# A fused attention and FP4 feed-forward kernel: semaphores per weight load, and the diagonal chunk of attention moved from first to last

## What is computed

```python
xn = _layernorm(x, axis=-1)
s = _L0_attn_ref(xn, Wq, bq, Wk, bk, Wv, bv, ln_g, ln_b, Wo, bo)
g = _silu(_L0_ffn_ref(xn, w_gate, w_up, w_down))
x = x + s * g
```

```python
def fp4_quant_dequant(x):                 # blocks of 16 along the last dim
    scale = jnp.maximum(jnp.max(jnp.abs(xb), axis=-1, keepdims=True) / 6.0, 1e-12)
    xn = xb / scale
    idx = jnp.searchsorted(_MID, jnp.abs(xn))       # 7 thresholds
    return (_GRID[idx] * jnp.sign(xn) * scale).reshape(shape)
gate = fp4_linear(x, w_gate);  y = fp4_linear(x, w_up)    # w_gate, w_up: [2816, 1024]
h = jax.nn.silu(gate) * y
return fp4_linear(h, w_down)                               # w_down: [1024, 2816]
```

## Time and profile before

| | us |
|---|---|
| median of 2 timed runs | 7727.67 |
| the two runs | 7749.9 and 7705.45 |
| the profiled execution, its own time | 7301.52 |
| span of its slowest core | 7299.9 |
| spans of its 8 cores | 7263.4 to 7299.9 |
| busy in that span: TensorE, VectorE, ScalarE, GpSimd | 3961.0, 2938.6, 798.3, 289.5 |
| mean granted TensorE clock of the cores (of 2.4 GHz) | 0.768 to 0.774 |

### The profile page before, as it was taken

How to read it: one execution, slowest core, us unless ns; L and a number is a source line. 1 busy time by engine, 2 the same in 40 slices (tenths; PEclk the granted TensorE clock), 3 DMA queues, 4 the chain that set the end, 5 groups by cost and what they waited for, 6 DMA issues and landing times.

```text
span 7299.9 us, 35941 instructions; the slowest of 8 cores (7263.4 to 7299.9 us)
## 1 busy us (share of the span) xinstructions
PE 3961.0 (54%) x10160; PEld 1770.9 (24%) x10160; DVE 2938.6 (40%) x7271; ACT 798.3 (11%) x1294; POOL 289.5 (4%) x420
## 2 busy tenths in 40 slices
PE   2600000000366774687577467857765688767746
PEld 1300000000122332232233223223332232223322
DVE  1177777777524562001456300033651000145630
ACT  1100000000030000023000002320000023300000
POOL 0000000000020000001000000100000000000000
PEclk9755555555688887798888778878887799988877
DMA  3110111011101111110111011002111200011102
GB/s 97 33 46 29 52 46 40 34 47 48 51 6 52 69 35 32 58 32 3 56 55 49 24 58 39 0 10 71 46 35 40 73 9 0 6 52 62 42 24 60
DMA packets 140128, 296.00 MB, mean 41 GB/s; under 512 B 10016, under 2 KB 77728, under 8 KB 139936
## 3 DMA queue, kind: packets, MB, share of 16 engines
q0 software_dynamic: 52480, 207.63, 8.6%
q1 hardware_dynamic: 87456, 86.08, 3.9%
HBM read 250.70 MB, written 42.99 MB: 40 GB/s over the span
## 4 chain that ended last, share of the span: by engine, by line
PE 43%; DVE 28%; DMA 10%; DVEq 6%; ACT 5%; issue 4%; ACTq 1%; POOL 1%; PEldq 1%; SPq 0%; PEld 0%; POOLq 0%
PE p L996 9%; PE p L950 6%; DVEq L83 6%; PE p L957 5%; PE p L709 5%; DMA ffnw<-wdq_s 4%; PE p L717 4%; PE p L854 3%; PE p L617 3%; PE p L657 3%; DMA xbuf<-x 3%; DVE qfm L280 3%; DVE qfm L285 2%; PE p L335 2%; PE p L383 2%
## 5 line engine op out<-in xcount | busy, mean ns | idle before, releaser
L950 PE MATMUL p<-ffnw,xnfm 128*128 128x512 f32 (+1 forms) x1536 | 722.2, 630 | 503.8 <-DMA ffnw<-wuq_s 317.0
L335 PE MATMUL p<-ident,hqfm 128*128 128x128 f32 (+1 forms) x592 | 133.7, 402 | 1457.6 <-DVE hqfm L306 1450.6
L996 PE MATMUL p<-hqfm,ffnw 128*128 128x512 f32 x1408 | 682.3, 648 | 340.8 <-DMA ffnw<-wdq_s 340.8
L957 PE MATMUL p<-ffnw,xnfm 128*128 128x512 f32 (+1 forms) x1536 | 620.2, 557 | 0.0
L724 DVE COPY ftmp<-p 65x512 f32<-65x512 f32 x32 | 22.0, 687 | 1397.4 <-PE p L717 1397.4
L950 PEld LDWEIGHTS p<-ffnw,xnfm 128*128 128x128 f32 x1536 | 331.1, 219 | 876.3 <-issue 865.7
L996 PEld LDWEIGHTS p<-hqfm,ffnw 128*128 128x128 f32 x1408 | 292.0, 210 | 729.4 <-issue 729.4
L335 PEld LDWEIGHTS p<-ident,hqfm 128*128 128x128 f32 (+1 forms) x592 | 103.5, 214 | 1488.2 <-issue 1483.4
L709 PE MATMUL p<-probs,vT 128*65 128x512 f32 x640 | 360.6, 716 | 151.9 <-POOL hqfm L686 79.2
L1009 DVE TENSOR_TENSOR sfm<-ftmp,sfm 128x512 f32<-128x512 f32 x32 | 22.1, 692 | 1005.2 <-ACTq L83 1005.2
L957 PEld LDWEIGHTS p<-ffnw,xnfm 128*128 128x128 f32 x1536 | 291.8, 190 | 312.7 <-issue 306.1
(11 more groups left out here) (153 smaller groups left out, 4908.7 us busy)
## 6 DMA issues: line engine op xcount, KB each, us to landing
ffnw<-wdq_s POOLq DMA_DIRECT2D x32, 1408.0 KB, 8.7
xbuf<-x SPq DMA_DIRECT2D x80, 512.0 KB, 4.0
ffnw<-wgq_s POOLq DMA_DIRECT2D x20, 2048.0 KB, 9.6
ffnw<-wuq_s POOLq DMA_DIRECT2D x20, 2048.0 KB, 14.1
ffnw<-Wq SPq DMA_DIRECT2D x32, 512.0 KB, 5.4
ffnw<-Wo SPq DMA_DIRECT2D x32, 512.0 KB, 4.4
hqfm<-wg POOLq DMA_DIRECT2D x22, 512.0 KB, 5.1
hqfm<-wu POOLq DMA_DIRECT2D x22, 512.0 KB, 4.9
```

The source lines that it names most:

```text
L335: E.do("tensor", lambda e, s=s, pb=pb, j=j, bp=bp, rows=rows: e.transpose(pb[:, j * rows:(j + 1) * rows], s, ident[bp:bp + rows, bp:bp + r ...
L950: E.do("tensor", lambda e, pg=pg, kc=kc, qt=qt, hw=hw: e.matmul(pg[:, 0:hw], xnfm[:, kc * 512 + qt * 128: kc * 512 + qt * 128 + 128], ffnw ...
L957: E.do("tensor", lambda e, pu=pu, kc=kc, qt=qt, hw=hw: e.matmul(pu[:, 0:hw], xnfm[:, kc * 512 + qt * 128: kc * 512 + qt * 128 + 128], ffnw ...
L996: E.do("tensor", lambda e, pd=pd, hc=hc: e.matmul(pd[:, 0:512], wdbuf[:, hc * 128:(hc + 1) * 128], hqfm[:, hc * 512:(hc + 1) * 512], start ...
```

## The change

Three edits.

1. In PW, both DMAs of unit k go on one of four semaphores (`qG`, `qG1` and two new ones, `qP0` and `qP1`), chosen by k mod 4, and the waits of ScalarE and VectorE ahead of unit k name that semaphore with the count kept at its own load.
2. For `wd`, both DMAs of tile oc go on `qG` (even) or `qG1` (odd), and the waits name that semaphore with the count of the tile's own load.
3. In the C stages the chunks run in ascending order, `for ch in range(qc + 1)`, so that the diagonal chunk is the last. `start` and `stop` of the AV accumulation and the waits for the free banks follow this order.

```diff
@@ -24,7 +24,7 @@
 HBS = [(0, 512), (512, 512), (1024, 512), (1536, 512), (2048, 512), (2560, 256)]
 R6 = float(np.float32(1.0) / np.float32(6.0))
 
-SEMS = ["qC", "qX0", "qX1", "qW0", "qW1", "qO0", "qO1", "qG", "qG1", "qGW", "qGW1",
+SEMS = ["qC", "qX0", "qX1", "qW0", "qW1", "qO0", "qO1", "qG", "qG1", "qP0", "qP1", "qGW", "qGW1",
         "t2v", "t2s", "t2g", "v2t", "v2s", "v2q", "v2g", "vv",
         "s2t", "s2v", "s2q", "s2g", "g2t"]
 
@@ -448,6 +448,8 @@
         qg_cnt = [0] * NU
         qg1_cnt = [0] * NU
 
+        SEM4 = ("qG", "qG1", "qP0", "qP1")
+
         def pw_load(k):
             w_src = units[k][0]
             h0, hw, hcl0 = units[k][3], units[k][4], units[k][5]
@@ -457,9 +459,8 @@
                 w_in = buf[:, ci * 1024:ci * 1024 + 1024]
                 E.do("gpsimd", lambda e, w_in=w_in, hc=hc, w_src=w_src: e.dma_start(
                     out=w_in, in_=w_src[hc * 128:(hc + 1) * 128, :]),
-                    sem=("qG" if ci == 0 else "qG1"), n=16)
-            qg_cnt[k] = E.c["qG"]
-            qg1_cnt[k] = E.c["qG1"]
+                    sem=SEM4[k % 4], n=16)
+            qg_cnt[k] = E.c[SEM4[k % 4]]
 
         for k in range(3):
             pw_load(k)
@@ -469,10 +470,8 @@
         for k in range(NU):
             w_src, w_dst, hb, h0, hw, hcl0 = units[k]
             buf = RING[k % 5]
-            E.wait("scalar", "qG")
-            E.wait("scalar", "qG1")
-            E.wait("vector", "qG")
-            E.wait("vector", "qG1")
+            E.wait("scalar", SEM4[k % 4], qg_cnt[k])
+            E.wait("vector", SEM4[k % 4], qg_cnt[k])
             quant_group(pw_items([buf[:, 0:1024], buf[:, 1024:2048]], 1024))
             E.wait("tensor", "v2s")
             wst = wstage_ab[wsa]
@@ -510,24 +509,23 @@
 
         def wd_load(oc):
             stag = wd_stag[oc % 2]
+            sm = "qG" if oc % 2 == 0 else "qG1"
             E.do("gpsimd", lambda e, oc=oc, stag=stag: e.dma_start(
                 out=stag[:, 0:1408], in_=wd[oc * 128:(oc + 1) * 128, 0:1408]),
-                sem="qG", n=16)
+                sem=sm, n=16)
             E.do("gpsimd", lambda e, oc=oc, stag=stag: e.dma_start(
                 out=stag[:, 1408:2816], in_=wd[oc * 128:(oc + 1) * 128, 1408:2816]),
-                sem="qG1", n=16)
-            wd_qg[oc] = E.c["qG"]
-            wd_qg1[oc] = E.c["qG1"]
+                sem=sm, n=16)
+            wd_qg[oc] = E.c[sm]
 
         E.wait("gpsimd", "t2g")
         wd_load(0)
         wd_load(1)
         for oc in range(NKC):
             stag = wd_stag[oc % 2]
-            E.wait("scalar", "qG")
-            E.wait("scalar", "qG1")
-            E.wait("vector", "qG")
-            E.wait("vector", "qG1")
+            sm = "qG" if oc % 2 == 0 else "qG1"
+            E.wait("scalar", sm, wd_qg[oc])
+            E.wait("vector", sm, wd_qg[oc])
             for grp in range(2):
                 subs = [stag[:, (grp * 2 + i) * 704:(grp * 2 + i + 1) * 704] for i in range(2)]
                 quant_group(pw_items(subs, 704))
@@ -642,12 +640,8 @@
                     hA = g * NKV + hkp
                     hB = hA + 1
                     chq = hA // 2
-                    ch_order = [qc] + list(range(qc))
-                    nch = len(ch_order)
-                    for ci, ch in enumerate(ch_order):
+                    for ch in range(qc + 1):
                         diag = ch == qc
-                        first = ci == 0
-                        last = ci == nch - 1
                         for j in range(4):
                             kc = ch * 4 + j
                             bA = SCA[j % 2]
@@ -700,26 +694,26 @@
                             E.wait("tensor", "g2t")
                         else:
                             E.wait("tensor", "s2t")
-                        if first:
+                        if ch == 0:
                             E.wait("tensor", av4_free[0][0], av4_free[0][1])
                             E.wait("tensor", av5_free[0][0], av5_free[0][1])
                         for j in range(4):
                             kc = ch * 4 + j
                             slot = (hkp * 16 + kc) * 65
-                            E.do("tensor", lambda e, j=j, slot=slot, first=first, last=last: e.matmul(
+                            E.do("tensor", lambda e, j=j, slot=slot, ch=ch: e.matmul(
                                 ps[4][0:65, 0:512],
                                 vT[:, slot:slot + 65],
                                 probs[:, j * 512:(j + 1) * 512],
-                                start=(first and j == 0), stop=(last and j == 3)))
+                                start=(ch == 0 and j == 0), stop=(diag and j == 3)))
                         for j in range(4):
                             kc = ch * 4 + j
                             slot = ((hkp + 1) * 16 + kc) * 65
-                            E.do("tensor", lambda e, j=j, slot=slot, first=first, last=last: e.matmul(
+                            E.do("tensor", lambda e, j=j, slot=slot, ch=ch, diag=diag: e.matmul(
                                 ps[5][0:65, 0:512],
                                 vT[:, slot:slot + 65],
                                 probsB[:, j * 512:(j + 1) * 512],
-                                start=(first and j == 0), stop=(last and j == 3)),
-                                sem=("t2v" if (last and j == 3) else None))
+                                start=(ch == 0 and j == 0), stop=(diag and j == 3)),
+                                sem=("t2v" if (diag and j == 3) else None))
                     E.wait("vector", "t2v")
                     E.do("vector", lambda e: e.tensor_copy(av_sbA[0:65, 0:512], ps[4][0:65, 0:512]),
                          sem="v2t")
```

## The result

| | before | changed |
|---|---|---|
| median of all timed runs, us | 7363.85 (10 runs) | 7375.13 (11 runs) |
| lowest and highest run | 7304.89, 7805.44 | 7129.47, 7685.45 |
| the profiled execution, its own time | 7301.52 | 7144.55 |
| ratio of comparable runs | | 0.9766, interval 0.9707 to 0.9826 |

Some executions of either kernel are stretched by up to 8% by a lower granted clock on one half of the chip's cores, so that the medians of all runs mix both kinds and hide the gain, while the ratio and the two profiled executions leave the stretched ones out. By the ratio the kernel is 2.3% faster, and since the interval reaches 0.9826, a gain of a little under 2% can't be excluded.

What follows compares the result with a forecast made beforehand. PW was taken as a serial loop in which each unit waits for a load just issued. Savings of 150.5 us (waits) and 13.6 us (chunk order), 164.1 in sum, off the 7727.7 us median gave 7563.6 us; range 7500 to 7640.

Steps and rivals of the forecast that it cites:

- The waits of the loads: In PW, each unit or `wd` tile waiting only for its own load was to save 150.5 us.
- Unit 0: First PW unit: Abs was to start near 344.3 instead of 349.71, no longer waiting for load 3; 5.4 us.
- Tile 0 of `wd`: First `wd` tile in PW: waiting for its own load instead of two was to save some 3.4 us.
- The chunk order: C1 to C3, diagonal chunk last: worth 0 by waits, a gain of 13.6 us by the granted clock.
- bounds +48 and -62: C1 to C3: C2's worst pattern in all 24 groups loses 48 us; all clock falls gone gains 62.
- full-clock groups: Groups of C1 to C3 without a clock fall were worked out as 29.81, 43.22 and 56.63 us.
- I let the fall of the even chunk go and keep the other: C2: the clock fall behind the 1.51 us stall goes, that behind the mask's 2.46 us stays; 8 x 1.70 us.
- C2's excess: C2: groups of 47.80 us against 43.22 at full clock, 4.58 us a group, 36.6 us over 8 groups.
- Clock worse in C: Rival, C stages: groups with one clock fall get two, leaving 102.5 us saved, 7625 us; chance 0.29.
- All falls gone: Rival, C1 to C3: every clock fall vanishes, saving 212.8 us in all, 7515 us; chance 0.06.
- GpSimd and VectorE collide: Rival, PW: DMA issues beside VectorE's units cost 50.2 us, leaving 114 saved, 7614 us; chance 0.05.
- Slower: Rival, C1 to C3: TensorE stays at 1.2 GHz through whole bursts, 7857 us with 40 of them; chance 0.02.

Runs made afterwards that it cites:

- loads_only: The changed kernel with its new semaphore waits on weight loads but the chunk loop of the kernel before; ratio 0.9814 to before, profiled execution 7226.0 us.
- all_three: The changed kernel plus useless matmuls filling the C stages' stalls and down-projection loads in two halves of `ffnw`; profiled execution 6770.7 us.
- two_newer: The changed kernel, with ScalarE and VectorE also waiting ahead of unit k for the load of unit k+2; execution 7606.6 us, PW 1445.5 us.

## Why the prediction was right or wrong

**The time itself was wrong, by its last step.** The range of 7500 to 7640 us missed the measured 7375.13. The step that failed is the one that took the saving off 7727.7: "The two timed runs have a median of 7727.7, 426 us above it, which no view explains". Of the ten runs of before, four lie above 7700, these two among them, and six between 7304.89 and 7369.17, beside the profiled execution's 7301.5. The other figure of the same paragraph, 7137 us on the scale of the profiled execution, has 7144.6 as its answer. Two timed runs that stand 5.5 and 6.1% above a profile are a warning that they are of another kind; a range on one of the two scales holds the time only by luck, and the saving of 164 us should have been put on the profile's. The median of all ten runs would not have saved the forecast: 7363.85 - 164.1 is 7199.8. Of the eleven runs after, six took 7375.13 us or more, so their median is set by how many of them are long, and not by the change.

**The saving was right.** Forecast 164.1, measured 156.9 between the two profiled executions; 0.9775 by the profile's scale, 0.9766 measured.

**The waits of the loads.** Forecast 150.5 us. Of it 145.1 fall behind the first Abs: measured -146.2, and -149 in loads_only. The period of a unit was to be 42.41 and is 42.25, that of a tile 60.70 and is 60.75. Unit 0 was to start some 0.37 us behind VectorE's last copy and not 5.8: its Abs starts at 346.07, and the copy ahead of it ends at 345.08 + 0.85 = 345.93. VectorE's timeline, changed kernel:

```profile
345.08 0.85 DVE L410 COPY vT<-p 128x256 f32<-128x256 f32 x2 [0.48 <-PE p L335]
```

The first row of the stage table doesn't show this, since the stages ahead of it vary more: their length is 331 to 377 us over the cores of all profiled executions. Tile 0 of `wd` gained 2.7 us for 3.4. The step that carried it, to take the price from the periods of the units that had no load left to wait for, and not from the idle sums of 845 us, is what the runs bear out.

**The chunk order.** Forecast 0 by waits and 13.6 us by the clock, bounds +48 and -62. Measured -12.2 in C2, -11.1 over C0 to C3, ratio 0.9946 alone. The size was met, and the full-clock groups (29.81, 43.22, 56.63) were met to 0.1 us once the stalls were filled. But the reason was wrong in one step: "I let the fall of the even chunk go and keep the other". It went the other way round. Of the 64 groups of C2 on the 8 cores, the burst behind the mask ran below full clock in all 64 before (46 of them took over 6 us in their first half) and in 20 after; a burst behind an even chunk's stall did so in 46 before and in 49 after, 47 of these at the group's first chunk. Over all bursts of the 64 groups there were 110 such falls in C2 and are 69 now, but 63 and 64 in C1, and 71 and 87 in C3, where 28 are still behind the mask. So the 13.6 us were met by luck: that C2 would gain and the others not followed from C2's excess, not from that reason.

**The rivals.** *Clock worse in C*: C3 gave back 3.5 us, no more. *All falls gone*: not by this change; the filled kernels show that it was a real bound, and reached it. *GpSimd and VectorE collide*: the issues last 1.05 us for two as before, land in 5.1 us, and end 1.64 us before VectorE starts; no collision. The rule of the Trainium skill on VectorE holding GpSimd's port (page "SBUF — State Buffer", section "SBUF: two separate sides") remains untested, since no load of PW is issued beside threshold comparisons in after either. *Slower*: no burst stayed at 1.2 GHz; the first half took at most 6.64 us for its 3.62.

**Open.** Why the old order settles in C2 in a pattern with two falls a group, and the new one in one with a single fall, came back in every kernel with that order (449 to 453 us in four, 438 to 440 in three) but was not explained. Whether the speed-up of all_three is at the cost of the chip's clock elsewhere is open too.

## What to carry to other kernels

A wait on a counter without a value means everything issued so far, and with loads issued ahead that is the one issued last; it undoes the prefetch it stands behind. Look at the distance from start to start, and compare units that still have a load ahead with those that have none: the difference is the price, whatever the idle sums say. A transfer must be old when it is waited for, so the target needs a second place before the wait can be moved. And where TensorE is stalled for 2 us at a time, matmuls without a use in the stall can be worth more than a better order of the useful ones.

## What was not expected of the hardware

- Stalls of 1.5 to 2.5 us between bursts went with a loss by the clock of almost half their own time. In C0 to C3 of the kernel before they are 151 us in all (8 groups each with 2.46, 3.97, 5.48 and 6.99 us), and with the stalls and the group boundaries filled these stages were 68 us shorter, though TensorE had more to do.
- The stall ahead of a burst depends on the chunk's place in the group as well as on its kind: 1.72 us for an even chunk (one without the mask) that is first and 1.51 for others, 2.46 for the masked chunk when first and 2.25 when last. The sum over a group is the same in both orders.
- In the down stages the clock came back with the waits: 129 us at 1.2 GHz a stage in the changed kernel, 49 with the loads in two halves. The blocks behind a wait took 20.6 to 22.2 us in the first such stage, against 18.9 at full clock.
- The clock records have a third level beside 1.00 and 0.50: 0.81, with 0 to 147 us a core in the profiles of before and of the changed kernel, and 3024 to 3553 us in that of two_newer, which took 7606.6 us.
